# The last four chunks of a mixture-of-experts combine, cut into eight parts, with GpSimd summing two of them

## The chip, the cores and the metric

One core of one Trainium2 chip runs the whole program. The metric is the device time of one execution in microseconds; the median of several runs counts.

## What is computed

The reference is one gated block over 128 sequences of 64 tokens with 128 features (8192 tokens): cross attention with 16 heads, added to x, and then a mixture of eight experts of which each token takes two, added again:

```python
x = x + jnp.tanh(g_xattn[0]) * _L0_xattn_ref(_layernorm(x), ctx_1024, ctx_1024, Wq, Wk, Wv, Wp, bp)
x = x + jnp.tanh(g_ffn[0]) * _L0_ffn_ref(_layernorm(x), gate_kernel, w0_kernel, w1_kernel, wo_kernel)
# _L0_ffn_ref: top 2 of 8 experts, softmax over the two, and
layer_mult = jax.nn.silu(layer_w0) * layer_w1
intermediate = jnp.einsum('blnh,nhe->blne', layer_mult, wo_kernel)
output = jnp.einsum('blne,bln->ble', intermediate, weights)
```

What the change touches is the last step alone: for every token the two weighted expert outputs are added to each other and to x.

## The kernel before

The tokens are 64 tiles of 128 (NT = 64). The first half of the program runs the attention tile by tile on all engines. For each tile GpSimd scatters the normalised rows, with indirect DMAs, into lists in HBM, one list per expert (`lists`, L1147), and the x after attention is copied into the resident tile `xres` (`keep`, L350, semaphores `x1_out`).

The second half goes over the lists in expert tiles of 256 rows: SP fetches them (`take`, L386), TensorE turns them and multiplies with the expert's weights, ScalarE and VectorE do the activation and the product, ScalarE scales the outputs (`ys`, L761), and GpSimd scatters the rows into `results` in HBM (L1203), two rows for each token, side by side. Each buffer of scatters has a semaphore, `y_out`.

The results come back in 16 chunks (NCHUNK) of four tiles (CHUNK = 4), each of 512 KB, into the four buffers of `yy`. A chunk takes three steps, on three engines:

- `fetch(k)` on SP (L401) waits until the buffer is free (`total_done`) and issues one DMA, `r_d` to `yy` (L404), with its own semaphore `y_in`.
- `combine(k)` on VectorE (L1054) adds the two rows of each token in `yy` (L1057, 128x512, both inputs in SBUF), waits for that, and adds the sum to `xres` (L1059, 128x512), which counts `total_done` up.
- `store(k)` on ScalarE (L765) waits for `total_done` and issues one DMA of 256 KB from `xres` to the output (L767).

The first twelve chunks (CHUNKS_EARLY = 12) belong to tokens whose results are all there some steps before the experts end; their steps are woven into the last steps of the expert pipeline. The last four can only be fetched when every scatter has landed: SP waits for all of `y_out` in `results_out(NET)` (L449) and then runs `fetch` for k = 12 to 15 (L450). VectorE, behind its expert pipeline, combines them in order (L1095), and ScalarE stores them in order and waits for all stores at the end (L808 to L810). GpSimd has nothing behind its last scatter (L1213).

Each engine runs its own instructions in order; the order above is written out by hand, and semaphores alone join the engines. DMAs from SP are in the profile's queue q1, those from ScalarE in q10, GpSimd's indirect ones in q0.

Of the kernel before, what the change touches and what calls it, by code (L numbers as in the profile page):

```python
# [9 lines left out]
ALU = mybir.AluOpType  # L10
# [6 lines left out]
NT = NB * S // P  # L17
# [72 lines left out]
EXPERTS = Pipeline(NET, behind=1, ahead=2, unroll=8, steady=18, turns=2)  # L90
SCATTERS = Pipeline(NET, behind=1, ahead=2, unroll=8, steady=26, turns=3)
CHUNK = 4
NCHUNK, CHUNKS_EARLY = NT // CHUNK, EARLY // CHUNK
COMBINE_AT = NET + 1 - CHUNKS_EARLY


def static(step, n):
# [12 lines left out]
def wait_slot(eng, sems, t, per, back=0):  # L110

    n = len(sems)
    lap = t.k // n + (0 if t.turn is None else t.turn * (t.unroll // n))
    v = per * (lap + 1 - back // n)
    if isinstance(v, int) and v <= 0:
        return
    eng.wait_ge(sems[t.buf(n)], v)
# [7 lines left out]
def flamingo_block(nc, A, out):  # L125
    with ExitStack() as ctx:
        def sb(name, shape, dt=F32):
            return ctx.enter_context(nc.sbuf_tensor(name, shape, dt))
# [4 lines left out]
        def sem(name):  # L133
            return ctx.enter_context(nc.semaphore(name))
# [95 lines left out]
        x1_out = [sem(f"x1_out{i}") for i in range(2)]  # L230
# [73 lines left out]
        def entry(t, h):  # L304
            if late(t):
                k = NFULL + 2 * (t.k - NFULL) + h
                return slice(k, k + 1)
            return slice(t.val, t.val + 1) if isinstance(t.val, int) else bass.ds(t.val, 1)

        def rows_there(eng, t):  # L310
# [4 lines left out]
            else:  # L315
                wait_slot(eng, z_in, t, 16)

        def expert(eng, t, h=0):

            return eng.value_load(table[0:1, 0, entry(t, h)], min_val=0, max_val=E - 1)  # L320


        yy = sb("yy", [P, 4, CHUNK, 2, D])
        y_in = [sem(f"y_in{i}") for i in range(4)]
        sum_done, total_done, out_done = sem("sum_done"), sem("total_done"), sem("out_done")
        EARLY_READY, LATE_READY = 11, 23
        r_d = results.rearrange("(c i p j) d -> p c i (j d)", j=2, i=CHUNK, p=P)
        xr_c = xres[:, :, :].rearrange("p (c i) d -> p c i d", i=CHUNK)
        o_c = o_d.rearrange("p (c i) d -> p c i d", i=CHUNK)

        with nc.Block() as block:
            @block.sync
            def _(sp):
# [67 lines left out]
                def fetch(k):  # L401
                    if k >= 4:
                        sp.wait_ge(total_done, k - 3)
                    sp.dma_start(yy[:, k % 4, :, :, :].rearrange("p i j d -> p i (j d)"), r_d[:, k, :, :]).then_inc(y_in[k % 4], 16)  # L404

                def results_out(tiles):
                    for i, n in enumerate(y_out):
                        sp.wait_ge(n, 32 * len(range(i, tiles, 8)))
# [38 lines left out]
                    if NEARLY + 8 + k < NET:  # L447
                        take(Tile(8, None, NEARLY + 8 + k))
                results_out(NET)  # L449
                for k in range(CHUNKS_EARLY, NCHUNK):  # L450
                    fetch(k)

            @block.tensor
            def _(pe):
# [132 lines left out]
                def second_layer(s):  # L587
                    if t := EXPERTS.at(s, 0):
                        e = [expert(pe, t, h) for h in range(2)] if late(t) else [expert(pe, t)] * 2
                        wait_for(pe, h_done, t)  # L590
                        wait_for(pe, y_sb, t, back=2)
                        if static(s, 3):
                            pe.wait_ge(place_done, NT)
                        if static(s, 7):
                            pe.wait_ge(late_table, 1)
                        for h in range(2):
                            for k in range(2):
                                last = pe.matmul(psY[t.buf(2)][:, h * D:(h + 1) * D], hm[:, t.buf(2), k, h * P:(h + 1) * P],  # L598
                                                 wo[:, bass.ds(e[h], 1), k, :].squeeze(1), start=(k == 0), stop=(k == 1))
                        last.then_inc(y_ps, 1)  # L600
# [64 lines left out]
            def _(act):  # L665
# [76 lines left out]
                def weights(s):  # L742
                    if t := EXPERTS.at(s, 2):
                        e = [expert(act, t, h) for h in range(2 if late(t) else 1)]
                        wait_for(act, b_ps, t, back=2)
                        for h, n in enumerate(e):
                            last = nc.scalar.copy(wcur[:, t.buf(2), h, :, :], w01[:, bass.ds(n, 1), :, :].squeeze(1))  # L747
                        last.then_inc(w_done, 1)
# [7 lines left out]
                def outputs(s):  # L756
                    if t := EXPERTS.at(s, 0):
                        wait_for(act, y_ps, t)
                        wait_slot(act, y_out, t, 32, back=8)
                        for h in range(2):  # L760
                            last = nc.scalar.activation(ys[:, t.buf(8), h, :], psY[t.buf(2)][:, h * D:(h + 1) * D], ACT.Copy,  # L761
                                                        scale=zin[:, t.buf(8), h, D + 1:D + 2])
                        last.then_inc(y_sb, 1)

                def store(k):  # L765
                    act.wait_ge(total_done, k + 1)
                    act.dma_start(o_c[:, k, :, :], xr_c[:, k, :, :]).then_inc(out_done, 16)  # L767

                def experts_step(s):
# [4 lines left out]
                    outputs(s)  # L774
                    if s[0] is None and s[1] > COMBINE_AT:
                        store(s[1] - COMBINE_AT - 1)

# [27 lines left out]
                        half_gaps(Tile(8, None, NT - 1))  # L805
                    normalised(Tile(8, None, NT - 4 + n))
                EXPERTS.run(act, experts_step, since=5)
                for k in range(CHUNKS_EARLY - 1, NCHUNK):  # L808
                    store(k)
                act.wait_ge(out_done, 16 * NCHUNK)  # L810

            @block.vector
            def _(dve):
# [232 lines left out]
                def products(s):  # L1046
                    if t := EXPERTS.at(s, 1):
                        wait_for(dve, b_ps, t)
                        wait_for(dve, silu_done, t)
                        wait_for(dve, y_ps, t, back=2)  # L1050
                        nc.vector.tensor_tensor(hm[:, t.buf(2), :, :].rearrange("p k t -> p (k t)"), psB[t.buf(2)][:, :], hs[:, t.buf(2), :],  # L1051
                                                ALU.mult).then_inc(h_done, 1)

                def combine(k):  # L1054
                    dve.wait_ge(y_in[k % 4], 16 * (k // 4 + 1))
                    ya, yb = yy[:, k % 4, :, 0, :], yy[:, k % 4, :, 1, :]
                    nc.vector.tensor_tensor(ya, ya, yb, ALU.add).then_inc(sum_done, 1)  # L1057
                    dve.wait_ge(sum_done, k + 1)
                    nc.vector.tensor_tensor(xr_c[:, k, :, :], xr_c[:, k, :, :], ya, ALU.add).then_inc(total_done, 1)  # L1059

                def experts_step(s):
# [3 lines left out]
                    products(s)  # L1065
                    if s[0] is None and s[1] >= COMBINE_AT:
                        if s[1] == COMBINE_AT:
                            for n in x1_out:
                                dve.wait_ge(n, 16 * (NT // 4))
                        combine(s[1] - COMBINE_AT)  # L1070

# [20 lines left out]
                experts_step((None, 3))  # L1092
                attention_step((None, NT + 1))
                EXPERTS.run(dve, experts_step, since=4)
                for k in range(CHUNKS_EARLY, NCHUNK):  # L1095
                    combine(k)

            @block.gpsimd
            def _(pool):
# [111 lines left out]
                    experts_step((None, n))  # L1211
                attention_step((None, NT))
                SCATTERS.run(pool, experts_step, since=4)  # L1213


# [36 lines left out]
```

## Time and profile before

| | us |
|---|---|
| median of three runs | 684.43 |
| lowest, highest | 681.34, 685.87 |
| span of the profiled execution, first to last instruction | 558.8 |
| median of the runs less that span | 125.6 |

The page gives the profiled execution's time as its span; the three runs are timed as a whole, with what lies around the first and the last instruction. The span is cut into stretches with the windows view: each line there gives the busy time of each engine within the stretch. Times are counted from the start of the span, and a row of the timeline gives start, length, engine, line, operation, output and input. "SPq" and "ACTq" are the issuing of DMAs by SP and ScalarE. A packet is one piece of a DMA: 1 KB in a fetch, 512 bytes in a store.

### The profile page before, as it was taken

To read this page: it belongs to the slowest core of one execution; us is meant where nothing else is said; L and a number is where in the kernel's file an instruction comes from. 1 tells how busy PE (TensorE), PEld (TensorE's weight loads), DVE (VectorE), ACT (ScalarE), POOL (GpSimd) and SP (SyncE) were. 2 spreads that over 40 slices of the span, in tenths; PEclk is the share of its full clock that TensorE was granted. 3 is DMA by queue.
4 is the path that set the end of the run, shared out by engine and by line. 5 is a ranking of instruction groups with operands and counts; after the bars stand their busy time and mean duration, and the time that the engine had idled before them with its cause. 6 is when DMAs were issued, how large, how long until landed. Compare 5 with 4: busy or idle time off the path is not lost.

```text
span 558.8 us, 20707 instructions
## 1 busy us (share of the span) xinstructions
PE 531.9 (95%) x6126; PEld 456.5 (82%) x6127; DVE 399.4 (71%) x1354; ACT 419.4 (75%) x1098; POOL 370.3 (66%) x516
## 2 busy tenths in 40 slices
PE   8999999999999999999999999999999999999950
PEld 6788888788888788878887778998889999999950
DVE  4789988988998898998899885466333333335763
ACT  3878888888888888888999886765556667777640
POOL 3127677676767767767767656777777777666560
PEclk9999999999999999999999999999999999999995
DMA  3642222121121121212212222224433333338987
GB/s 90 196 119 79 60 67 74 52 85 57 52 80 57 59 73 62 80 52 71 75 55 75 63 77 71 85 88 132 127 102 106 103 105 99 92 104 257 320 265 226
DMA packets 72945, 57.17 MB, mean 102 GB/s; under 512 B 9119, under 2 KB 68768, under 8 KB 72880
## 3 DMA queue, kind: packets, MB, share of 16 engines
q1 hardware_dynamic: 55552, 35.05, 22.4%
q0 software_dynamic: 8448, 16.93, 9.1%
q10 hardware_dynamic: 8880, 4.39, 2.7%
q8 instruction: 32, 0.52, 0.4%
q14 instruction: 33, 0.27, 0.2%
HBM read 29.44 MB, written 23.22 MB: 94 GB/s over the span
## 4 chain that ended last, share of the span: by engine, by line
PE 86%; ACT 3%; issue 3%; DMA 3%; ACTq 2%; DVE 2%; POOL 1%; POOLq 0%; SPq 0%; DVEq 0%
PE psH L582 17%; PE psO L551 12%; PE psH L491 12%; PE psH L477 7%; PE psH L483 7%; PE psK L529 5%; PE psG L598 4%; PE psO L598 4%; PE psO L509 3%; PE psX L496 3%; PE psO L523 3%; ACTq L320 1%; PE psX L533 1%; PE psK L504 1%; PE psX L534 1%
## 5 line engine op out<-in xcount | busy, mean ns | idle before, releaser
L1147 POOL DMA_INDIRECT lists<-zp,dest x128 | 128.1, 1001 | 61.4 <-DVE dest L951 31.1
L1203 POOL DMA_INDIRECT results<-ys,zin x136 | 133.8, 984 | 52.2 <-issue 42.1
L582 PE MATMUL psH<-zT,wcur 128*128 128x128 f32 (+1 forms) x760 | 131.0, 321 | 1.1 <-issue 0.7
L582 PEld LDWEIGHTS psH<-zT,wcur 128*128 128x128 f32 x760 | 109.5, 191 | 8.9 <-issue 1.1
L1051 DVE TENSOR_TENSOR hm<-psH,hs 128x512 f32<-128x512 f32 x68 | 47.0, 691 | 91.7 <-PE psH L582 46.6
L684 ACT ACTIVATE ex<-psH,rs 128x512 f32<-128x512 f32 x128 | 81.2, 684 | 38.8 <-PE psH L483 38.8
L936 DVE TENSOR_REDUCE mx<-psH 128x8 fp32r<-128x512 f32 x128 | 82.5, 686 | 4.4 <-PE psH L477 0.3
L551 PEld LDWEIGHTS psO<-v,pT 128*64 128x64 f32 x2048 | 64.9, 138 | 25.1 <-issue 23.5
L491 PE MATMUL psH<-ident,ex 128*128 128x128 f32 x512 | 76.4, 282 | 0.1
L551 PE MATMUL psO<-v,pT 128*64 128x64 f32 x2048 | 73.7, 225 | 0.6 <-ACT pT L688 0.6
L747 ACT COPY wcur<-w 128x512 f32 x95 | 56.0, 616 | 23.9 <-issue 19.3
L1186 POOL TENSOR_TENSOR kvr<-ropA,ropB 128x256 f32<-128x256 f32 x64 | 46.5, 726 | 41.1 <-DVE ropB L1013 24.6
L688 ACT COPY pT<-psH 128x512 f32<-128x512 f32 x128 | 72.9, 600 | 0.2
L728 ACT COPY v<-kvr 64x64 f32<-64x64 f32 x256 | 63.3, 247 | 2.2
L491 PEld LDWEIGHTS psH<-ident,ex 128*128 128x128 f32 x512 | 54.0, 140 | 13.2 <-ACT ex L684 10.1
L483 PE MATMUL psH<-mx,minus 128*128 128x256 f32 x256 | 59.8, 320 | 0.0
L961 DVE TENSOR_TENSOR kmask<-psK,hmask 128x512 f32<-128x512 f32 x64 | 44.0, 687 | 3.0 <-PE psK L504 2.4
L477 PE MATMUL psH<-kmask,qT 32*64 32x256 f32 x1024 | 44.6, 400 | 0.0
L754 ACT ACTIVATE hs<-psH 128x512 f32<-128x512 f32 x68 | 40.2, 591 | 3.4 <-PE psH L582 3.3
L483 PEld LDWEIGHTS psH<-mx,minus 128*128 128x128 f32 x256 | 38.5, 190 | 3.6 <-DVE mx L936 0.2
L529 PE MATMUL psK<-wT,xcT 128*128 128x256 f32 x128 | 38.7, 384 | 1.1 <-DVE kmask L961 1.1
L678 ACT ACTIVATE zp<-x1r,nmr,rs 128x256 f32<-128x256 f32 x64 | 38.5, 602 | 1.5
(163 smaller groups left out, 951.8 us busy)
## 6 DMA issues: line engine op xcount, KB each, us to landing
yy<-results SPq DMA_DIRECT2D x16, 512.0 KB, 5.2
zin<-lists SPq DMA_DIRECT2D x41, 130.0 KB
xres<-x1r SPq DMA_DIRECT2D x32, 128.0 KB, 2.2
out_dram<-xres ACTq DMA_DIRECT2D x16, 256.0 KB
xring<-in_x_dram SPq DMA_DIRECT2D x31, 128.0 KB, 2.2
cring<-in_ctx_dram SPq DMA_DIRECT2D x31, 128.0 KB, 2.4
zin<-lists SPq DMA_DIRECT2D x54, 65.0 KB
results<-ys,zin POOLq DMA_INDIRECT x136
```

The lines of the kernel that those rows point to most:

```text
L477: last = pe.matmul(psH[h][c, g % 2, 0:256], qT[r, t.buf(2), c], kmask[r, t.buf(2), :, c], start=True, stop=False, skip_group_check=True)
L483: last = pe.matmul(psH[h][:, g % 2, 0:256], minus[:, :], mx[:, 4 * g:4 * g + 4].unsqueeze(2).broadcast_to([P, 4, S]), start=False, stop=Tr ...
L491: last = pe.transpose(psH[h][:, n // 2, o:o + P], ex[:, t.buf(2), h, n * P:(n + 1) * P], ident[:, :])
L529: pe.matmul(psK[:, 0:2 * D], xcT[:, t.buf(8), P:2 * P], wT[:, 1:3, :], start=True, stop=True).then_inc(kv_ps, 1)
L551: last = pe.matmul(psO[b * S:(b + 1) * S, n * VW:n * VW + VPAD], pT[:, t.buf(2), n // 4, o:o + S], v9[:, t.buf(4), b, n * VW:n * VW + VPAD ...
L582: last = pe.matmul(bank[t.buf(2)][:, k * ET + c.start:k * ET + c.stop], wcur[:, t.buf(2), h, a, k * P:(k + 1) * P], zT[:, t.buf(2), c], st ...
L684: nc.scalar.activation(ex[:, t.buf(2), h, :].rearrange("p (g c) -> p g c", g=2), psH[h][:, :, 0:256], ACT.Exp, scale=rs[:, t.buf(4) // 2, ...
L688: nc.scalar.copy(pT[:, t.buf(2), h, :].rearrange("p (g c) -> p g c", g=2), psH[h][:, :, 256:512]).then_inc(p_sb[h], 1)
L728: last = nc.scalar.copy(dst, src)
L936: nc.vector.tensor_reduce(mx[:, 8 * h:8 * h + 8].rearrange("p (g n) -> p g n", g=2), psH[h][:, :, 0:256].rearrange("p g (n k) -> p g n k", ...
L1147: nc.gpsimd.indirect_dma_start(lists, bass.IndirectOffsetOnAxis(ap=dest[:, t.buf(4), j:j + 1], axis=0), zp[:, t.buf(4), j, :], None).then_ ...
L1203: nc.gpsimd.indirect_dma_start(results, bass.IndirectOffsetOnAxis(ap=zin[:, t.buf(8), h, D:D + 1].bitcast(U32), axis=0), ys[:, t.buf(8), h ...
```

## The change

The last four chunks are fetched, summed and stored in eight parts (LAST = 8) of two tiles (PART = 2). Part n is tiles 0 and 1, or 2 and 3, of chunk 12 + n // 2. SP issues eight fetches of 256 KB, each with its own semaphore `half_in`. VectorE sums parts 0, 1, 3, 4, 6 and 7 with additions of 128x256; GpSimd sums parts 2 and 5 with the same two additions, behind its last scatter and a wait for the copies of x. ScalarE stores the eight parts in order, 128 KB each, when `half_total` of the part is there. The early chunks are unchanged.

```diff
--- before.py
+++ after.py
@@ -90,8 +90,11 @@
 EXPERTS = Pipeline(NET, behind=1, ahead=2, unroll=8, steady=18, turns=2)
 SCATTERS = Pipeline(NET, behind=1, ahead=2, unroll=8, steady=26, turns=3)
 CHUNK = 4
+PART = CHUNK // 2
 NCHUNK, CHUNKS_EARLY = NT // CHUNK, EARLY // CHUNK
 COMBINE_AT = NET + 1 - CHUNKS_EARLY
+LAST = 2 * (NCHUNK - CHUNKS_EARLY)
+POOL_PARTS = (2, 5)
 
 
 def static(step, n):
@@ -315,6 +318,11 @@
             else:
                 wait_slot(eng, z_in, t, 16)
 
+        def part(n):
+
+            k, i = CHUNKS_EARLY + n // 2, n % 2 * PART
+            return k, slice(i, i + PART)
+
         def expert(eng, t, h=0):
 
             return eng.value_load(table[0:1, 0, entry(t, h)], min_val=0, max_val=E - 1)
@@ -323,6 +331,9 @@
         yy = sb("yy", [P, 4, CHUNK, 2, D])
         y_in = [sem(f"y_in{i}") for i in range(4)]
         sum_done, total_done, out_done = sem("sum_done"), sem("total_done"), sem("out_done")
+        half_in = [sem(f"half_in{i}") for i in range(LAST)]
+        half_sum = [sem(f"half_sum{i}") for i in range(LAST)]
+        half_total = [sem(f"half_total{i}") for i in range(LAST)]
         EARLY_READY, LATE_READY = 11, 23
         r_d = results.rearrange("(c i p j) d -> p c i (j d)", j=2, i=CHUNK, p=P)
         xr_c = xres[:, :, :].rearrange("p (c i) d -> p c i d", i=CHUNK)
@@ -447,8 +458,11 @@
                     if NEARLY + 8 + k < NET:
                         take(Tile(8, None, NEARLY + 8 + k))
                 results_out(NET)
-                for k in range(CHUNKS_EARLY, NCHUNK):
-                    fetch(k)
+                for n in range(LAST):
+                    if n % 2 == 0:
+                        sp.wait_ge(total_done, CHUNKS_EARLY + n // 2 - 3)
+                    k, tiles = part(n)
+                    sp.dma_start(yy[:, k % 4, tiles, :, :].rearrange("p i j d -> p i (j d)"), r_d[:, k, tiles, :]).then_inc(half_in[n], 16)
 
             @block.tensor
             def _(pe):
@@ -805,9 +819,12 @@
                         half_gaps(Tile(8, None, NT - 1))
                     normalised(Tile(8, None, NT - 4 + n))
                 EXPERTS.run(act, experts_step, since=5)
-                for k in range(CHUNKS_EARLY - 1, NCHUNK):
-                    store(k)
-                act.wait_ge(out_done, 16 * NCHUNK)
+                store(CHUNKS_EARLY - 1)
+                for n in range(LAST):
+                    act.wait_ge(half_total[n], 1)
+                    k, tiles = part(n)
+                    act.dma_start(o_c[:, k, tiles, :], xr_c[:, k, tiles, :]).then_inc(out_done, 16)
+                act.wait_ge(out_done, 16 * (CHUNKS_EARLY + LAST))
 
             @block.vector
             def _(dve):
@@ -1092,8 +1109,14 @@
                 experts_step((None, 3))
                 attention_step((None, NT + 1))
                 EXPERTS.run(dve, experts_step, since=4)
-                for k in range(CHUNKS_EARLY, NCHUNK):
-                    combine(k)
+                for n in range(LAST):
+                    if n not in POOL_PARTS:
+                        k, tiles = part(n)
+                        dve.wait_ge(half_in[n], 16)
+                        ya, yb, xa = yy[:, k % 4, tiles, 0, :], yy[:, k % 4, tiles, 1, :], xr_c[:, k, tiles, :]
+                        nc.vector.tensor_tensor(ya, ya, yb, ALU.add).then_inc(half_sum[n], 1)
+                        dve.wait_ge(half_sum[n], 1)
+                        nc.vector.tensor_tensor(xa, xa, ya, ALU.add).then_inc(half_total[n], 1)
 
             @block.gpsimd
             def _(pool):
@@ -1211,6 +1234,15 @@
                     experts_step((None, n))
                 attention_step((None, NT))
                 SCATTERS.run(pool, experts_step, since=4)
+                for n in x1_out:
+                    pool.wait_ge(n, 16 * (NT // 4))
+                for n in POOL_PARTS:
+                    k, tiles = part(n)
+                    pool.wait_ge(half_in[n], 16)
+                    ya, yb, xa = yy[:, k % 4, tiles, 0, :], yy[:, k % 4, tiles, 1, :], xr_c[:, k, tiles, :]
+                    nc.gpsimd.tensor_tensor(ya, ya, yb, ALU.add).then_inc(half_sum[n], 1)
+                    pool.wait_ge(half_sum[n], 1)
+                    nc.gpsimd.tensor_tensor(xa, xa, ya, ALU.add).then_inc(half_total[n], 1)
 
 
 # ---- launch: one core; inputs and outputs as the reference has them ----
```

## Rows read from the trace of the kernel before

**Rows 1.** The page: span, and the chain that ended last by engine.
```profile
span 558.8 us, 20707 instructions
...
PE 86%; ACT 3%; issue 3%; DMA 3%; ACTq 2%; DVE 2%; POOL 1%; POOLq 0%; SPq 0%; DVEq 0%
```

**Rows 2.** Windows of the tail: length, busy per engine, clock, DMA share, GB/s.
```profile
546.30:550.20 3.90, 0.00 (x0) 0.00 (x0) 0.00 (x0) 0.00 (x0) 0.00 (x0) 0.50 0.61 210
550.20:556.10 5.90, 0.00 (x0) 0.00 (x0) 5.54 (x8) 0.00 (x0) 0.00 (x0) 0.50 1.06 330
556.10:558.80 2.70, 0.00 (x0) 0.00 (x0) 0.00 (x0) 0.00 (x0) 0.00 (x0) 0.50 0.48 142
```

**Rows 3.** The chain in order of time, from 540: start, us, what.
```profile
543.90 2.22 DMA results<-ys,zin
...
546.32 0.36 SPq L404
...
547.82 6.82 DMA yy<-results
```

**Rows 4.** Timeline of the tail.
```profile
550.20 0.69 DVE L1057 TENSOR_TENSOR yy<-yy 128x512 f32<-128x512 f32 x1 [8.01 <-DMA yy<-results]
...
551.65 4.85 ACTq L767 DMA_DIRECT2D out_dram<-xres  x4
551.71 0.69 DVE L1057 TENSOR_TENSOR yy<-yy 128x512 f32<-128x512 f32 x1
...
554.67 0.69 DVE L1057 TENSOR_TENSOR yy<-yy 128x512 f32<-128x512 f32 x1
...
556.12 0.39 ACTq L767 DMA_DIRECT2D out_dram<-xres  x1
```

**Rows 5.** Issues of fetches and stores: ns min/median/max.
```profile
L404 SPq DMA_DIRECT2D yy<-results x16: 359/432/525, 500.5 to 547.8; - x16
...
L767 ACTq DMA_DIRECT2D out_dram<-xres x16: 387/387/501, 513.0 to 556.1; - x16
```

**Rows 6.** Groups of instructions, shapes apart: busy us, mean ns, idle before.
```profile
L1010 DVE TENSOR_TENSOR ropA<-psK,cosT 128x256 f32<-128x256 f32 x64 | 27.1, 423 | 7.5 <-PE psK L529 3.7
...
L1004 DVE TENSOR_TENSOR x1r<-psO,bpg 128x136 f32<-128x136 f32 x64 | 19.0, 297 | 14.5 <-PE psO L523 14.0
...
L1059 DVE TENSOR_TENSOR xres<-xres,yy 128x512 f32<-128x512 f32 x16 | 11.1, 694 | 0.6
...
L1186 POOL TENSOR_TENSOR kvr<-ropA,ropB 128x256 f32<-128x256 f32 x64 | 46.5, 726 | 41.1 <-DVE ropB L1013 24.6 <-ACT v L728 15.9 <-issue 0.2
```

**Rows 7.** Timeline in the attention half, GpSimd and VectorE.
```profile
153.30 0.24 POOL L1168 TENSOR_SCALAR ve<-mv 128x4 f32<-128x4 f32 x1
153.69 1.05 POOL L1170 TENSOR_TENSOR rs<-ve,mhalf 128x4 f32<-128x4 f32 x1
154.73 0.72 POOL L1186 TENSOR_TENSOR kvr<-ropA,ropB 128x256 f32<-128x256 f32 x1
...
154.29 1.29 DVE L936 TENSOR_REDUCE mx<-psH 128x8 fp32r<-128x512 f32 x2
```

**Rows 8.** DMA from 545 to 559: all packets; stores (packets, MB, share).
```profile
DMA packets 4276, 3.16 MB, mean 225 GB/s; under 512 B 163, under 2 KB 4276, under 8 KB 4276
...
q10 hardware_dynamic: 2130, 1.06, 25.2%
```

**Rows 9.** The stores' queue from 553 to 554.
```profile
q10 hardware_dynamic: 96, 0.05, 16.7%
```

**Rows 10.** The stores' queue from 554 to 555.
```profile
q10 hardware_dynamic: 677, 0.34, 112.7%
```

**Rows 11.** The stores' queue from 556.6 to 557.1.
```profile
q10 hardware_dynamic: 18, 0.01, 5.9%
```

**Rows 12.** The stores' queue from 553.2 to 553.6.
```profile
q10 hardware_dynamic: 4, 0.00, 1.8%
```

**Rows 13.** The stores' queue from 557 to 558.
```profile
q10 hardware_dynamic: 516, 0.26, 86.1%
```

## The prediction

> **What bounds the kernel now.** The page comes first: 558.8 us of span, and a chain that ended last which is 86% TensorE and only 3% DMA [rows 1]. So nearly all of the span is a stream of matmuls that the change doesn't touch, and the question is how long the stretch behind the last matmul is. The windows by stage, the second view, answer it: from 546.3 on TensorE, ScalarE and GpSimd are idle; from 546.3 to 550.2 nothing but the DMA engines work, from 550.2 to 556.1 VectorE is busy for 5.54 of 5.90 us while the DMA share is at 1.06, and in the last 2.7 us only DMAs run again [rows 2]. That is 12.5 us in which the change can act, 1.8% of 684.43.
>
> The chain in order of time says who holds the end [rows 3]. The last indirect scatter of results is issued at 543.90 and lands 2.22 us later; SP has waited for it, and issues its four last fetches from 546.32 on; the fourth, issued at 547.82, lands 6.82 us later, at 554.6, and releases the last pair of additions. The timeline shows the same from VectorE's side [rows 4]: the first pair starts at 550.20, the second at 551.71, the last at 554.67. A pair is 0.69 + 0.69 us and two gaps, 1.45; chunks land every (554.67 - 550.20) / 3 = 1.49 us. So VectorE and the transfers go at one pace, and the reader is to see that neither alone is the bound: VectorE's sum just fits between two landings, and the chain passes through the fourth landing. The last store is issued at 556.12, and the span ends 2.7 us after it.
>
> **What is not touched.** The scatters, the release at 546.3, the bytes (four chunks of 512 KB in, four of 256 KB out), the size of the single packets, and the early chunks stay. Beside the work, 24 semaphores and some 20 instructions are new; against 20707 instructions [rows 1] this is a tenth of a per cent. Nothing in the trace shows what the time around the span (684.43 - 558.8 = 125.6 us) is made of; if all of it went with the number of instructions, a tenth of a per cent of it would be 0.1 us either way. I take 0.
>
> **Issues of the fetches.** SP issues eight instead of four. An issue takes 0.36 to 0.53 us [rows 5], (547.82 - 546.32) / 3 = 0.5 from one to the next [rows 3], so the last one goes out at about 546.32 + 7 x 0.53 = 550.0. One part is half a chunk, 0.73 us of transfer; by 550.0 only part 0, and hardly part 1, has landed. The queue is never empty, and the four added issues are hidden behind transfers. Without that cover (if a smaller DMA were much quicker to move than to issue) the cost would be below 8 x 0.53 - 8 x 0.73, less than nothing: 0. The wait for a free buffer, once per chunk as before, asks for totals of early chunks, and VectorE is done with them by 546.3 [rows 2]; GpSimd's added wait for the copies of x asks for transfers that ended in the attention half. Both cost 0, and behind GpSimd's wait there is only its own pair of parts.
>
> **First sum.** Part 0 has 256 packets fewer in front of its landing than chunk 0, half of 1.49 us: it lands at 549.5 instead of 550.2. Parts then land at 549.5, 550.2, 551.0, 551.7, 552.4 as long as no store mixes in.
>
> **Sums.** VectorE's addition of 128x256 with both inputs in SBUF isn't in the trace. The nearest rows: 128x512 with the same operands 0.69 us, 128x256 with one input in PSUM 0.42, 128x136 0.30 [rows 6]; the line through them gives 0.42. The bounds are half of 0.69 (0.35) and 0.69. A pair costs 2 x 0.42 + 0.06 = 0.9 on VectorE. GpSimd's 128x256 addition took 0.73 us [rows 6] and a dependent GpSimd instruction starts 0.15 us behind the one that it waits for [rows 7]: a pair is 1.6 us. VectorE has six pairs, 5.4 us, for parts that take eight times 0.73 = 5.8 us to land; GpSimd has 3.2 us for two, three parts (2.2 us) apart. Without a coupling of the two both are ahead of the landings. Part 2 is done at 551.0 + 1.6 = 552.6, when part 3 is done as well (551.7 + 0.9), so ScalarE, which stores in order, hardly waits for it; the same holds for part 5. With all eight on VectorE it would be 8 x 0.9 = 7.2 us from 549.5, until 556.7: GpSimd's share is what keeps twice as many instructions from being late.
>
> **Stores and what they collide with.** This is the term that eats the gain. Before, the first store was issued at 551.65 [rows 4] and of all 2130 packets of stores [rows 8] only 96 had moved when 554.0 came [rows 9]; then the fetches were through and the stores had the engines: 677 packets a us [rows 10], 0.38 us for the 256 packets of a part. Now part 0 is summed at 550.4, part 1 at 551.3, parts 2 and 3 near 552.6, and each is stored at once (an issue on ScalarE 0.39 to 0.50 us [rows 5]). From issue to first packets it took about 1 us on an idle queue (556.12 to 557.1, where 18 packets had gone [rows 11]) and 1.6 or more under load (issued at 551.65, and four packets of it had gone in the window from 553.2 to 553.6 [rows 12]). So stores 0 and 1 and most of store 2 come between the last fetches: 2 to 3 times 0.38 us is 0.76 to 1.14, less the 96 packets of before (0.14): the last fetch lands 0.6 to 1.0 later, I take 0.8, at 555.5 instead of 554.67. Bounds: 0, if the queues were served in order of issue, and 1.4, if four stores got in.
>
> **The end.** Part 7 lands at 555.5, when part 6 is nearly summed; its pair ends at 556.4 to 556.5, against 556.08 before: 0.4 later. Its store moves 128 KB instead of 256. Of the 2.7 us from issue to the end, data moved for about one (516 packets between 557 and 558 [rows 13]); half of that goes, 0.5. 556.5 + 2.2 = 558.7; with the first half of the landing delay, 0.6, it is 558.5. I take 558.6, 0.2 us less than 558.8. Not one of these sums reaches a thousandth of the time.
>
> **The Trainium skill.** The rows show GpSimd's 128x256 addition beside VectorE's maxima, which read PSUM, at 0.72 us, no longer than its mean of 0.726 [rows 6, 7]; no row shows one beside a VectorE addition that has both inputs in SBUF, and that is what the changed tail has. By the Trainium skill, "SBUF — State Buffer", section "Who interferes with whom", a VectorE instruction with two SBUF inputs and a GpSimd instruction that reads SBUF exclude each other: the second one blocks until the first is through. By that rule the result would be the second rival's instead of mine.
>
> **Rivals.** First, the finer grain gives all that it can: the stores don't hold up the fetches. Part 7 lands at 554.67, is summed by 555.6, and 2.2 us on the span ends at 557.8, 1.0 less. For it speaks that the engines were also busy before (share 1.06 [rows 2]) and still took 96 packets without visible delay; against it, that a full engine can't move more. 683.4 us.
>
> Second, the other side: VectorE and GpSimd take turns. From 549.5 on, 12 VectorE additions of 0.42 (5.0 us) and four of GpSimd of 0.73 (2.9) go one after another, 7.9 us, with gaps of 0.03 to 0.15 where one hands over to the next about 8.3: the last total is ready at 557.8, the store ends 2.2 later at 560.0, 1.2 us more than before. It decides only from the point where additions queue, from part 2 on, and turns the bound from transfers to additions. For it: every operand is in SBUF. Against it: no row. 685.6 us.
>
> Third, a small fetch isn't overlapped with the next: 549.5 - 546.3 = 3.2 us each, 8 x 3.2 = 25.6 us, and the additions end at 572.8, 16.7 later: 701 us. Against it: four fetches in the queue land 1.49 us apart though the first took 3.9; transfers flow into each other.
>
> Fourth, the change doesn't do what it says: GpSimd's two parts relieve an engine that isn't late, as landings set the pace. That is inside my forecast; alone it is worth nothing either way.
>
> **How the numbers follow.** Forecast, stores held against fetches: 0.45, 684.43 - 0.2 = 684.2. All of the gain: 0.17, 683.4. Turns: 0.33, 685.6. No overlap of small fetches, or something that no row shows, around the span too: 0.05. The likeliest alone has 683.3 to 685.0. The terms are smaller than the scatter of the runs shown (681.34 to 685.87 about a median of 684.43), which sets the range: 681.3 to 687.0, the upper end the turns' time and 1.4 of that scatter. A measurement of this kernel can tell about 1%, 6.8 us, from no change. Faster by more would ask for half of the 12.5 us, while 3.16 MB [rows 8] must still move at some 330 GB/s [rows 2], 9.6 us: 0.01. Slower by more comes from the last case alone: 0.02. Within 1%: 0.97.
>
> **What would show it.** Right: first addition near 549.5, first store near 550.4, packets of stores mixed with the fetches' from 552 on, the last landing between 555.2 and 555.7, GpSimd's additions at 0.73 and VectorE's at 0.42, the last store issued near 556.5. Wrong: additions of VectorE or GpSimd stretched or starting only as the other ends (the second rival), a last landing at 554.7 (the first), or a gap in the DMA share between parts (the third). The forecast falls as a whole if the span before 546.3 moves by more than the tail does.

## The result and the profile after

| | before | changed |
|---|---|---|
| median of 20 runs, us | 682.25 | 687.97 |
| ratio, 95% interval | | 1.0089 (1.0061 to 1.0116) |
| span of the profiled run, us | 558.8 | 682.9 |
| time of that run, us | not given | 684.87 |

The change makes the kernel slower by 0.9%, some 6 us. The forecast was 0.2 us faster, 684.2, within 681.3 to 687.0; the measured time lies outside, on the other side, though within the 1% that the chances called "the same".

The two spans can't be compared as wholes. The changed kernel's run took 684.87 us for a span of 682.9: about 2 us lie around a span, and not 125.6. The page of the kernel before fits an execution on a faster chip than that of the 20 runs: its chip isn't on record, but a later run (e8_before_again) gave the same kernel 561.33 us with a span of 559.3. The experiments fell on three chips: e1 to e4 on one where the kernel before takes 682 us, e5 to e8 and e9 to e12 on two where it takes 562. Each ratio below compares runs of one chip. The ratios leave disturbed executions out; the traces of e2_pool_first, e3_late_memset and e4_late_wait are of such slower ones (689.58, 693.34 and 688.87 us), but in their tails VectorE's addition alone takes 0.42 or 0.69 us as in the others. What follows is therefore counted from one instant that every trace has: the issue of the first late fetch, at 546.32 us in the trace of before and at 663.78 in the changed kernel's. From there to the end of the span it is 12.5 us before and 19.1 after.

The page of the changed kernel, its span and the engines of the chain. That the chain is 58% TensorE here and 86% before is the slower chip, and not the change: the same changed kernel has 88% on a fast one (e9_changed_again).

```profile
span 682.9 us, 20724 instructions
...
PE 58%; another core or an unknown queue 12%; issue 10%; ACT 9%; DVE 4%; ACTq 3%; POOL 1%; DMA 1%; DVEq 1%; SPq 0%; POOLq 0%
```

The windows of the changed tail, with the columns of [rows 2]: from the first late fetch to the last addition, to the last store's landing, and to the end.

```profile
663.80:674.70 10.90, 0.00 (x0) 0.00 (x0) 5.75 (x12) 0.00 (x0) 3.39 (x4) 0.50 0.83 255
674.70:676.80 2.10, 0.00 (x0) 0.00 (x0) 0.00 (x0) 0.00 (x0) 0.00 (x0) 0.50 0.62 173
676.80:682.90 6.10, 0.00 (x0) 0.00 (x0) 0.00 (x0) 0.00 (x0) 0.00 (x0) 0.50 0.00 0
```

The last line is the finding: 6.1 us in which no engine is busy and no DMA moves a byte, and the program isn't over. A busy-time view can't say why. The instructions of the line that opens the block (L342 here, L331 before) can: they are each engine's last ones, a DRAIN and the joining of the engines. Columns: line, engine's queue, operation, count, ns min/median/max, first and last start. The changed kernel:

```profile
L342 POOLq EVENT_SEMAPHORE  x2: 17/17/17, 682.7 to 682.8; - x2
...
L342 POOLq DRAIN  x1: 9575/9575/9575, 672.8 to 672.8; - x1
L342 DVEq DRAIN  x1: 464/464/464, 674.3 to 674.3; - x1
...
L342 ACTq DRAIN  x1: 8/8/8, 676.8 to 676.8; - x1
```

And the same rows of the kernel before, of its first trace:

```profile
L331 POOLq EVENT_SEMAPHORE  x2: 17/17/17, 558.7 to 558.7; - x2
...
L331 POOLq DRAIN  x1: 11415/11415/11415, 542.2 to 542.2; - x1
...
L331 ACTq DRAIN  x1: 8/8/8, 558.6 to 558.6; - x1
```

GpSimd's DRAIN starts at 672.80 and ends 9.58 later at 682.38, and the joining follows within 0.5 us. ScalarE, which waits for the last store, had been through since 676.8. Before, the DRAIN took even longer, 11.4 us, but it started at 542.19, when GpSimd still had scatters to work off, and ended at 553.6: 5 us before ScalarE was through, so it cost nothing. In both traces it ends 8.7 to 8.8 us after GpSimd's last work (544.87 and 673.62). The two parts of GpSimd moved that instant to 9.84 us after the first late fetch.

The timeline of the changed tail shows a second thing, as [rows 4] did for before:

```profile
663.78 3.95 SPq L465 DMA_DIRECT2D yy<-results  x8
666.51 0.43 DVE L1117 TENSOR_TENSOR yy<-yy 128x256 f32<-128x256 f32 x1 [6.70 <-DMA yy<-results]
...
669.35 0.72 POOL L1243 TENSOR_TENSOR yy<-yy 128x256 f32<-128x256 f32 x1 [6.86 <-DMA yy<-results]
670.10 0.42 DVE L1117 TENSOR_TENSOR yy<-yy 128x256 f32<-128x256 f32 x1 [1.90 <-DMA yy<-results]
670.14 0.96 POOL L1245 TENSOR_TENSOR xres<-xres,yy 128x256 f32<-128x256 f32 x1
670.55 0.83 DVE L1119 TENSOR_TENSOR xres<-xres,yy 128x256 f32<-128x256 f32 x1
671.31 0.41 DVE L1117 TENSOR_TENSOR yy<-yy 128x256 f32<-128x256 f32 x1
...
671.83 0.93 POOL L1243 TENSOR_TENSOR yy<-yy 128x256 f32<-128x256 f32 x1 [0.73 <-DMA yy<-results]
672.50 0.54 DVE L1117 TENSOR_TENSOR yy<-yy 128x256 f32<-128x256 f32 x1 [0.32 <-DMA yy<-results]
672.84 0.78 POOL L1245 TENSOR_TENSOR xres<-xres,yy 128x256 f32<-128x256 f32 x1
673.08 0.83 DVE L1119 TENSOR_TENSOR xres<-xres,yy 128x256 f32<-128x256 f32 x1
```

Where an addition of GpSimd and one of VectorE overlap, the later one is stretched: VectorE's 0.42 becomes 0.83, GpSimd's 0.72 becomes up to 0.96. And part 2 lands late: VectorE is idle for 1.90 us between parts 1 and 3. The last addition ends 10.9 us after the first late fetch, against 9.8 before.

### The profile page after: what moved, and what is told of

It reads as the page before. It is cut to its first block, busy times and chain, and to the rows that moved or that the text cites. A ratio compares the mean times of both kernels' runs of the same rounds, so it can differ in the third digit from the quotient of the medians.

```text
span 682.9 us, 20724 instructions
## 1 busy us (share of the span) xinstructions
PE 571.1 (84%) x6126; PEld 471.9 (69%) x6127; DVE 400.1 (59%) x1358; ACT 420.8 (62%) x1098; POOL 376.3 (55%) x520
## 4 chain that ended last, share of the span: by engine, by line
PE 58%; another core or an unknown queue 12%; issue 10%; ACT 9%; DVE 4%; ACTq 3%; POOL 1%; DMA 1%; DVEq 1%; SPq 0%; POOLq 0%
PE psO L565 10%; PE psH L505 8%; PE psH L491 7%; PE psH L497 6%; PE psH L596 6%; PE psK L543 4%; ACT wcur L761 3%; PE psO L523 3%; PE psG L528 2%; PE psO L537 2%; ACT ys L775 2%; ACTq L328 2%; ACT hs L768 2%; PE psX L510 2%
## 5 line engine op out<-in xcount | busy, mean ns | idle before, releaser
L596 PE MATMUL psH<-zT,wcur 128*128 128x128 f32 (+1 forms) x760 | 136.6, 329 | 24.4 <-ACT wcur L761 17.0
L596 PEld LDWEIGHTS psH<-zT,wcur 128*128 128x128 f32 x760 | 111.6, 194 | 38.3 <-ACT wcur L761 19.9
L698 ACT ACTIVATE ex<-psH,rs 128x512 f32<-128x512 f32 x128 | 83.4, 685 | 77.9 <-PE psH L497 54.1
L565 PEld LDWEIGHTS psO<-v,pT 128*64 128x64 f32 x2048 | 67.8, 137 | 34.2 <-issue 33.4
L565 PE MATMUL psO<-v,pT 128*64 128x64 f32 x2048 | 78.1, 226 | 7.6 <-issue 7.6
L505 PEld LDWEIGHTS psH<-ident,ex 128*128 128x128 f32 x512 | 56.4, 142 | 16.6 <-ACT ex L698 12.3
L775 ACT ACTIVATE ys<-psO,zin 128x128 f32<-128x128 f32 x68 | 21.2, 363 | 66.0 <-remote 50.7
L768 ACT ACTIVATE hs<-psH 128x512 f32<-128x512 f32 x68 | 40.6, 598 | 23.4 <-PE psH L596 11.8
L491 PE MATMUL psH<-kmask,qT 32*64 32x256 f32 x1024 | 50.0, 407 | 2.1 <-ACT pT L702 2.0
L612 PE MATMUL psG<-wo,hm 128*128 x272 | 38.6, 286 | 15.3 <-DVE hm L1068 14.1
L612 PEld LDWEIGHTS psG<-wo,hm 128*128 128x128 f32 x272 | 35.1, 195 | 20.2 <-issue 19.3
```

The costliest lines, as they stand in the source:

```text
L491: last = pe.matmul(psH[h][c, g % 2, 0:256], qT[r, t.buf(2), c], kmask[r, t.buf(2), :, c], start=True, stop=False, skip_group_check=True)
L505: last = pe.transpose(psH[h][:, n // 2, o:o + P], ex[:, t.buf(2), h, n * P:(n + 1) * P], ident[:, :])
L565: last = pe.matmul(psO[b * S:(b + 1) * S, n * VW:n * VW + VPAD], pT[:, t.buf(2), n // 4, o:o + S], v9[:, t.buf(4), b, n * VW:n * VW + VPAD ...
L596: last = pe.matmul(bank[t.buf(2)][:, k * ET + c.start:k * ET + c.stop], wcur[:, t.buf(2), h, a, k * P:(k + 1) * P], zT[:, t.buf(2), c], st ...
L698: nc.scalar.activation(ex[:, t.buf(2), h, :].rearrange("p (g c) -> p g c", g=2), psH[h][:, :, 0:256], ACT.Exp, scale=rs[:, t.buf(4) // 2, ...
```

## The experiments

The theory: GpSimd's closing DRAIN takes some 8.7 us from its last work, it was hidden, and the change puts work behind which it no longer is. Rival A: VectorE and GpSimd block each other, and that is the cost. Rival B: the loss lies ahead of the tail.

All times below are us after the first late fetch's issue, from each run's trace. The last column is called the stretch in what follows.

| run | GpSimd's last work ends | DRAIN ends | last addition ends | stores waited for until | end |
|---|---|---|---|---|---|
| before | -1.5 | 7.3 | 9.8 | 12.3 | 12.5 |
| changed | 9.8 | 18.6 | 10.9 | 13.0 | 19.1 |
| e1_split_vector | -1.3 | 7.4 | 10.2 | 12.3 | 12.5 |
| e2_pool_first | 4.6 | 13.3 | 10.3 | 12.3 | 13.5 |
| e3_late_memset | 8.5 | 17.3 | 9.8 | 12.3 | 17.5 |
| e4_late_wait | a wait, to 8.5 | 17.3 | 9.8 | 12.4 | 17.5 |
| e5_early_drain | 8.4 | 8.5 | 9.7 | 12.3 | 12.5 |
| e6_write_only | 8.9 | 17.7 | 10.6 | 12.8 | 18.2 |
| e7_after_early_drain | 11.0 | 11.1 | 11.8 | 14.2 | 14.4 |
| e8_before_again | -1.3 | 7.4 | 9.7 | 12.3 | 12.5 |
| e9_changed_again | 9.9 | 18.6 | 11.4 | 13.5 | 19.2 |
| e10_mid_drain | a wait, to 8.6 | 17.5 | 10.0 | 12.6 | 17.7 |
| e11_split_vector_again | -1.3 | 7.4 | 10.4 | 12.5 | 12.7 |
| e12_last_chunk_halved | -1.3 | 7.4 | 9.9 | 12.0 | 12.2 |

**e1_split_vector**: eight parts, without GpSimd.

```diff
-POOL_PARTS = (2, 5)
+POOL_PARTS = ()
```

> The changed kernel with all eight parts summed by VectorE; GpSimd does nothing behind its last scatter. Theory (GpSimd's closing DRAIN ends 8.7 to 8.8 us after GpSimd's last work, and that is what ends the program): the DRAIN ends some 5 us before the end again, as before, the stretch from the first late fetch's issue to the end is 12 to 12.7 us instead of 19.1, and the time is 0.99 to 1.00 of before. Rival A (VectorE and GpSimd block each other, and that is the cost): the stretch falls only by the 1.2 us by which the last addition was later, to about 18. Rival B (the loss lies in the stages before the tail): the stretch is shorter, but the time stays near 1.009 of before.

Measured: 683.12 us, ratio 1.0026 (0.9989 to 1.0062), stretch 12.5. The 6.6 us are gone with GpSimd's two parts. Rival A would have left 18; rival B would have left a ratio of 1.009 and is out too. That VectorE ends 0.4 later than before and the store takes 0.4 less is as in the forecast.

**e2_pool_first**: GpSimd sums the part that lands first.

```diff
-POOL_PARTS = (2, 5)
+POOL_PARTS = (0,)
```

> The changed kernel with GpSimd summing part 0 alone, VectorE the other seven. Theory: GpSimd's last addition ends about 4.5 us after the first late fetch's issue (3.2 to land, 0.72 + 0.15 + 0.72 to sum, less what the first fetch lands earlier), the DRAIN ends 8.8 us after that, 13 to 13.6 us after the issue, and the whole stretch is 13.2 to 13.8 us against 12.5 before and 19.1 changed; time 1.000 to 1.003 of before. Rival A (mutual blocking is the cost): about 12.3, since VectorE is idle while part 0 is summed. Rival (any GpSimd compute after its scatters costs a fixed amount, wherever it is): 18 to 19.

Measured: stretch 13.5, ratio 0.9964 (0.9922 to 1.0007). GpSimd's last addition ends at 4.57 and its DRAIN at 13.32, 8.76 later, only 1.0 after ScalarE is through. So the cost moves with the instant of the last work; it is no fixed price of computing on GpSimd. One us can't be told from the ratio on this chip.

**e3_late_memset** and **e4_late_wait**: the kernel before, with a wait behind GpSimd's last scatter; e3 has a memset of one column behind the wait, as below; e4 has the wait alone.

```diff
                 SCATTERS.run(pool, experts_step, since=4)
+                pool.wait_ge(total_done, NCHUNK - 1)
+                nc.gpsimd.memset(zeros[:, 0:1], 0.0)
```

> The kernel before with one GpSimd memset of 128x1 that waits for the third of the last four totals; nothing else is changed. Theory: the memset at about 8.4 us after the first late fetch's issue, DRAIN ends 8.7 us after it, and the stretch is 17.1 to 17.4 us, 4.6 to 4.9 more than before; time 1.006 to 1.008 of before. Rival A (mutual blocking): nothing reads beside VectorE, so 12.5 and 1.000. Rival B (GpSimd's additions themselves are the cost): 12.5 and 1.000.

> The kernel before with only the wait of the last run on GpSimd, and no instruction behind it. It parts two forms of the theory: if the 8.7 us run from the DRAIN's own start, the DRAIN is started at 8.4 us after the first late fetch's issue and ends near 17.2 (time 1.006 to 1.008 of before); if they run from GpSimd's last work, the last scatter, they are long over and the DRAIN ends at once (12.5 and 1.000).

Measured: e3 ratio 1.0095 (1.0047 to 1.0142), stretch 17.5; e4 1.0068 (1.0011 to 1.0125), stretch 17.5. The two intervals overlap, and 5 us of 682 (1.0073) lies in both. The rows of e4_late_wait:

```profile
L331 POOLq COMPARE_BRANCH  x1: 38/38/38, 677.8 to 677.8; - x1
L331 POOLq DRAIN  x1: 8730/8730/8730, 678.0 to 678.0; - x1
L331 DVEq DRAIN  x1: 730/730/730, 678.5 to 678.5; - x1
L331 ACTq COMPARE_BRANCH  x1: 38/38/38, 681.6 to 681.6; - x1
L331 ACTq DRAIN  x1: 8/8/8, 681.7 to 681.7; - x1
```

No addition of GpSimd is there, nothing blocks VectorE, and a bare wait costs 5 us. The 8.73 us run from the DRAIN's own start, even 10 us after GpSimd's last scatter. So the DRAIN isn't waiting for a transfer: GpSimd's scatters had landed at least 8.6 us before it began, and it ends at 17.3, 5 us after the last store. What it does in that time no view shows.

**e5_early_drain**: e3 with an explicit drain behind the last scatter.

```diff
                 SCATTERS.run(pool, experts_step, since=4)
+                nc.gpsimd.drain()
                 pool.wait_ge(total_done, NCHUNK - 1)
                 nc.gpsimd.memset(zeros[:, 0:1], 0.0)
```

> The kernel of e3_late_memset with an explicit drain on GpSimd right behind its last scatter, ahead of the wait and the memset. If the 8.7 us are spent on something that a first drain settles (entries of its indirect DMAs, say), the closing DRAIN is short, the stretch from the first late fetch's issue to the end is 12.5 us and the time 1.000 of before. If every DRAIN of GpSimd costs 8.7 us whatever went before, the stretch stays at 17.3 and the time at 1.006 to 1.009.

Measured, on a faster chip: 561.83 us, ratio 0.9999 (0.9980 to 1.0018), stretch 12.5. First the explicit drain, then the closing one:

```profile
L1214 POOLq DRAIN  x1: 11327/11327/11327, 543.3 to 543.3; - x1
```

```profile
L331 POOLq DRAIN  x1: 168/168/168, 555.5 to 555.5; - x1
```

The long part is paid once: with no indirect DMA issued since the first, the second DRAIN takes 0.17 us. Put where it is hidden, it takes the whole cost of the late instruction away. That the indirect DMAs are what makes a DRAIN long is likely but not shown: GpSimd's DRAIN at the very start of the program, before any of them, took 0.17 us too (0.4 us into the trace of before), but no run leaves them out and keeps GpSimd's other work of the expert loop.

**e6_write_only**: the changed kernel, GpSimd's four additions replaced by memsets (parts 2 and 5 are left unsummed).

```diff
-                    nc.gpsimd.tensor_tensor(ya, ya, yb, ALU.add).then_inc(half_sum[n], 1)
+                    nc.gpsimd.memset(ya, 0.0).then_inc(half_sum[n], 1)
                     pool.wait_ge(half_sum[n], 1)
-                    nc.gpsimd.tensor_tensor(xa, xa, ya, ALU.add).then_inc(half_total[n], 1)
+                    nc.gpsimd.memset(yb, 0.0).then_inc(half_total[n], 1)
```

> The changed kernel with GpSimd's four additions replaced by memsets of the same 128x256 tiles, so that GpSimd only writes (parts 2 and 5 are left unsummed). Theory of blocking by the reads: every addition of VectorE takes 0.42 to 0.43 us, where the changed kernel has two of 0.83; GpSimd's last work ends 0.5 to 0.8 us earlier and the stretch is about 18.3 to 18.6 (the closing DRAIN still ends it). Rival (any work of GpSimd in SBUF beside VectorE stretches it): some additions of VectorE stay near 0.8.

Measured: ratio 1.0095 (1.0076 to 1.0114), stretch 18.2, just under what was expected, as GpSimd's last work ended 0.9 us earlier and not 0.5 to 0.8. VectorE's additions in e6_write_only, ns min/median/max:

```profile
L1117 DVE TENSOR_TENSOR yy<-yy x6: 418/425/426, 550.7 to 557.7; 128x256 f32<-128x256 f32 x6
L1119 DVE TENSOR_TENSOR xres<-xres,yy x6: 424/424/426, 551.2 to 558.2; 128x256 f32<-128x256 f32 x6
```

No addition is stretched, where the changed kernel has maxima of 541 and 828. In this run no memset happened to overlap an addition, though: the first ends at 554.17, 0.06 after VectorE has started, and the others fall into its gaps. So the run doesn't part the two: it shows only that an addition with nothing of GpSimd's beside it takes 0.42. The traces of e3 and e5 say more. Theirs is a memset of one column that falls inside an addition of VectorE; in e3_late_memset:

```profile
682.27 0.69 DVE L1057 TENSOR_TENSOR yy<-yy 128x512 f32<-128x512 f32 x1
682.31 0.10 POOL L1215 MEMSET zeros<- 128x1 f32 x1 [9.92 <-DVE xres L1059]
```

The memset is through after 0.10 us, 0.55 before the addition is, and the addition keeps its 0.69; in e5_early_drain it is the same. So a GpSimd instruction that only writes doesn't wait for such an addition, at least a small one; a large one was not seen beside an addition. The last addition of e6 ends 0.3 us earlier than in the changed kernel, which is about what the turns cost at the end.

**e7_after_early_drain**: the changed kernel with the explicit drain of e5.

```diff
                 SCATTERS.run(pool, experts_step, since=4)
+                nc.gpsimd.drain()
                 for n in x1_out:
```

> The changed kernel with an explicit drain on GpSimd behind its last scatter. It ends about 7.3 us after the first late fetch's issue, so GpSimd's two parts are summed from 7.3 to about 10.8 instead of ending at 9.8. If a first drain makes the closing one short, the stretch is about 14; if each costs 8.7 us, it is 19.5 to 20.5 and the time about 1.010 of before.

Measured: 562.63 us, ratio 1.0014 (0.9996 to 1.0031), stretch 14.4. With the long DRAIN out of the way the loss falls from 6.6 us to 1.9, and that rest has its own reason: the early drain holds GpSimd until 7.4, so parts 2 and 5 are summed late and side by side with VectorE's. In e7_after_early_drain three pairs in a row take turns:

```profile
554.32 0.78 POOL L1246 TENSOR_TENSOR xres<-xres,yy 128x256 f32<-128x256 f32 x1
554.68 0.70 DVE L1117 TENSOR_TENSOR yy<-yy 128x256 f32<-128x256 f32 x1 [0.16 <-DMA yy<-results]
555.07 0.90 POOL L1244 TENSOR_TENSOR yy<-yy 128x256 f32<-128x256 f32 x1
555.42 0.83 DVE L1119 TENSOR_TENSOR xres<-xres,yy 128x256 f32<-128x256 f32 x1
556.04 0.78 POOL L1246 TENSOR_TENSOR xres<-xres,yy 128x256 f32<-128x256 f32 x1
556.17 0.94 DVE L1117 TENSOR_TENSOR yy<-yy 128x256 f32<-128x256 f32 x1
```

VectorE's addition from 554.68 ends at 555.38, 0.28 after GpSimd's from 554.32; the one from 555.42 ends at 556.25, again 0.28 after GpSimd's. In each pair the instruction that started later is the one that ends later than it would alone: one engine is held until the other is nearly through.

**e8_before_again**: no edit.

> The kernel before against itself: ratio 1.000 with an interval of some 0.4% on either side, and a second profile of it. The stretch from the first late fetch's issue to the end is 12.5 us again with GpSimd's DRAIN over some 5 us earlier. The span tells whether 558.8 us was typical: every other profile here has a span 2 us below its run's time (682.9 for 684.87), so I expect about 680, with the difference in idle time of the loops, and not in the tail.

Measured: ratio 0.9986 (0.9969 to 1.0002), span 559.3, stretch 12.5. The expectation about the span was wrong for this chip (559.3, not 680) and right in its rule (time less span 2.0 us). It gives back the page of before: the 125.6 us "around the span" were the difference of two chips.

**e9_changed_again**: no edit to the changed kernel.

> The changed kernel again, beside the others of this call on one chip. On either of the two chips seen so far (one gives the kernel before 682, the other 562 us) the loss is the same in us: 6 to 7, so 1.009 to 1.010 on the first and 1.011 to 1.0125 on the second, with a stretch of 19 us from the first late fetch's issue to the end. If the loss came from the stages before the tail, it would be a share and not an amount.

Measured on a fast chip: 567.43 us, ratio 1.0094 (1.0076 to 1.0112), stretch 19.2. The share came out under what I expected: 1.0094 of 562 is 5.3 us (4.3 to 6.3), where the stretches differ by 6.7. So the amount is about the same on both chips, but some of it, of the order of 1 us, isn't accounted for; the profiled run, at 570.65, was the slowest of its five (the others 567.29 to 568.80).

**e10_mid_drain**: e4 with a drain in the middle.

```diff
+                nc.gpsimd.drain()
                 SCATTERS.run(pool, experts_step, since=4)
+                pool.wait_ge(total_done, NCHUNK - 1)
```

> The kernel of e4_late_wait with an explicit drain on GpSimd ahead of its expert loop, about half of its 264 indirect DMAs before it. If a DRAIN's length goes with the number of indirect DMAs since the last one (8.73 us for all, 33 ns each), the closing DRAIN takes 4.3 to 5.0 us, and so does the first; the program then ends 12.9 to 13.7 us after the first late fetch's issue. If it is one amount for any number, it takes 8.7 and the stretch is 17.3. The drain in the middle may cost some us of its own there, so the time tells less than the stretch.

Measured: ratio 1.0171 (1.0136 to 1.0205), stretch 17.7. The middle drain, then the closing one:

```profile
L1213 POOLq DRAIN  x1: 7236/7236/7236, 351.1 to 351.1; - x1
```

```profile
L331 POOLq DRAIN  x1: 8719/8719/8719, 557.9 to 557.9; - x1
```

The count theory falls: with only the 138 indirect DMAs issued since the middle one, the closing DRAIN takes 8.72 us, as with all 264. The middle one ended at 358.3, only 2.1 us after GpSimd's last work before it (at 356.2), though 126 indirect DMAs lay before it. So not every DRAIN behind indirect DMAs takes 8.7 us, and what sets the length stays open. The ratio means 9.6 us, of which the tail explains 5.2; the rest fell before the tail, probably where the middle drain held GpSimd up, as the expectation had allowed.

**e11_split_vector_again** and **e12_last_chunk_halved**: the search for a version that beats both. e12 splits the last chunk alone, on VectorE:

```diff
-                for k in range(CHUNKS_EARLY, NCHUNK):
+                for k in range(CHUNKS_EARLY, NCHUNK - 1):
                     combine(k)
+                for h in range(2):
+                    i = slice(2 * h, 2 * h + 2)
+                    dve.wait_ge(half_in[h], 16)
+                    ya, yb, xa = yy[:, 3, i, 0, :], yy[:, 3, i, 1, :], xr_c[:, NCHUNK - 1, i, :]
+                    nc.vector.tensor_tensor(ya, ya, yb, ALU.add).then_inc(half_sum, 1)
+                    dve.wait_ge(half_sum, h + 1)
+                    nc.vector.tensor_tensor(xa, xa, ya, ALU.add).then_inc(half_total, 1)
...
```

> The kernel of e1_split_vector again, on the chip of the changed kernel: the eight parts without GpSimd. Stretch 12.4 to 12.7 us, time 0.998 to 1.002 of before: the finer grain by itself gives nothing, since twelve more instructions on VectorE (16 additions of 0.42 against 8 of 0.69, and a late third part) take back what the earlier first landing and the smaller last store give.

> The kernel before with only the last chunk in two halves, all on VectorE. Chunks 12 to 14 are summed as before, by 8.3 us after the first late fetch's issue; the halves' sums end at about 9.2 and 10.1 (9.8 before), and the last store of 128 KB takes 2.1 instead of 2.5 us: stretch 12.2 to 12.5 us, time 0.998 to 1.001 of before, nothing that can be told from it.

(Sixteen additions against eight are eight more instructions, not the twelve of e11's expectation.) Measured: e11 1.0009 (0.9991 to 1.0026), stretch 12.7; e12 0.9994 (0.9977 to 1.0012), stretch 12.2. Neither differs measurably from before; e12's trace is 0.3 us shorter, in what both the store (2.1 us from the last addition to ScalarE's release, 2.5 before) and the sums (0.1 later) lead one to expect.

Part of why eight small fetches give nothing is in the windows. Both lines are the stretch from 4.0 to 7.0 us after the first late fetch, in e8_before_again and in e11_split_vector_again:

```profile
550.86:553.86 3.00, 0.00 (x0) 0.00 (x0) 2.76 (x5) 0.00 (x0) 0.00 (x0) 0.50 1.10 349
```

```profile
551.76:554.76 3.00, 0.00 (x0) 0.00 (x0) 2.05 (x6) 0.00 (x0) 0.00 (x0) 0.50 0.89 263
```

The DMAs move 263 GB/s instead of 349, and VectorE waits. In e12, with three fetches whole, the same stretch had 349 again. All traces agree in the direction: the seven with whole fetches ahead in this stretch moved 348 to 350 GB/s there, the seven with eight small ones 248 to 326. Among these the amount varies widely (263 in e11_split_vector_again and 295 in e1_split_vector, the same kernel), so a quarter is one case and not a rule.

## Why the prediction was wrong

- **The step that failed** is in "Issues of the fetches", where GpSimd's new wait was costed at 0 because "behind GpSimd's wait there is only its own pair of parts", and in "The end", which lets the program end 2.2 us behind the last sum, with the last store. The description of the kernel before has the same error: GpSimd has something behind its last scatter. Behind GpSimd's parts stands its closing DRAIN of 8.7 us, and the program ends with the last engine. Before, its cover was 5.0 us of the tail (over at 7.3, needed at 12.3); a GpSimd instruction that ends later than 3.6 us after the first late fetch takes the end over. The changed one ends at 9.8, so the DRAIN is over at 18.6, 6.3 us after the old 12.3, and from there to the end the joining of the engines takes 0.3 us longer than before: together the 6.6 us. e1, e3, e4 and e5 show it by taking the parts away, by putting a bare wait in their place, and by paying the DRAIN early. The row was in the trace of before, under the block's own line, and the chain even passed through its first 1.40 us; I read the views of busy time, which leave DRAINs out.
- **The time around the span**: 2 us, not 125.6. It entered the sum as 0, so it cost nothing, but two executions, most likely of different chips, were taken for one.
- **The turns of VectorE and GpSimd** (second rival) are real: additions of 0.83 beside 0.78 to 0.96. The forecast gave it 0.33 and priced the end 1.2 us later; the stores were through 0.7 to 1.2 us later than before, but for the most part because the last fetch landed late (below): VectorE took up the last part 0.25 us after it had landed. By the Trainium skill, "SBUF — State Buffer", section "Who interferes with whom", the second of the two blocks until the first is through: the traces agree as far as additions against additions go. But the turns have only a small part in the path that sets the end. It runs through GpSimd's last two additions, 0.93 and 0.78 us for 0.72 each, so without turns the DRAIN would have started working some 0.3 us earlier (an estimate from these rows); the turns that held VectorE cost nothing.
- **The sums**: 0.42 us for 128x256 on VectorE, as predicted from the line through three rows; GpSimd 0.72 alone, where 0.73 was predicted. The first landing came at 2.7 us, not 3.2; the third part's sum began at 5.6, where its landing was put at 4.7. Landings were not evenly 0.73 us apart.
- **Stores against fetches**: this term was too small. The last landing was to be 0.8 us later than before, within bounds of 0 and 1.4, at 9.2 after the first late fetch. The rows of the eight issues in the changed trace settle it: the last one started at 667.3, and the longest way to landing, 6.3 us, can only be its own, since every other part was summed less than 5.8 us after its issue. So it landed at 9.8, 1.5 us later than before (8.3). The reason given, stores between the fetches, is at best a part: from 1.5 to 5.0 us after the first late fetch only the fetches' queue had packets, 1071 of them in the changed kernel and 1161 in e8_before_again, so the rate had dipped before any store moved. Small fetches against whole ones (e11 against e12) are what the runs tell apart, not the cause within the DMA engines.

```profile
L465 SPq DMA_DIRECT2D yy<-results x8: 360/468/472, 663.8 to 667.3; - x8
...
DMA to landing us min/median/max: 2.7/5.0/6.3
```

- **The third rival** (no overlap of small fetches) was wrong as priced, 16.7 us, and small fetches do overlap; but its direction was right: they moved 7% to 29% less than whole ones in the 3 us above.

## What to carry to other kernels

Before work is put on an idle engine at the end of a kernel, look at what that engine still has to do after its last instruction: here GpSimd, which had issued indirect DMAs, needed a DRAIN of 8.7 us, and an instruction on it that came late, even a wait, moved the whole end. If the work must be there, an explicit drain behind the last indirect DMA pays that amount where it is hidden (1.0014 on one fast chip, where the changed kernel without it had 1.0094 on another). It made the kernel no faster than before. And where a span and a time are far apart, ask whether they come from one execution before the difference is called overhead.

## What the runs showed of the hardware

- GpSimd's first DRAIN behind the last indirect DMA: 8.72 to 8.76 us from GpSimd's last work, or from its own start if that is later, in all fourteen traces, on at least three chips, with 264 or 138 indirect DMAs since the last drain; a closing one behind it took 0.17 us (e5) or ended 0.07 after the last addition (e7). A drain issued between indirect DMAs, at 351 us, took only 2.1 us beyond GpSimd's last work.
- The same program took 682 us on one chip and 562 on two others; the changed kernel's tail was 19.1 and 19.2 us. For the changed kernel TensorE was busy for 571 us on the slow one and for 532 on a fast one, and the slow one's chain has 12% put down to another core or an unknown queue. The cause stays open.
- VectorE's addition of 0.42 us with both inputs in SBUF took up to 0.94 beside GpSimd's, and GpSimd's of 0.72 up to 0.96; a GpSimd memset of 128x1 inside VectorE's 128x512 addition changed neither (0.10 and 0.69).
- From 4 to 7 us after the first late fetch, eight fetches of 256 KB moved 248 to 326 GB/s (seven traces), where 512 KB fetches moved 348 to 350 (seven traces).
